# A switch-routed layer in one launch: the tokens at the boundary of two experts handled in blocks of 128 instead of 256

## What is computed

```python
xn = _layernorm(x)                                   # x: 8 x 512 x 512, that is 4096 tokens
s = attention(xn)                                    # 16 heads, causal, alibi bias
logits = x_flat @ w_router.T                         # 2 experts
top_idx = jnp.argmax(probs, axis=-1)
h = jnp.einsum('nd,ehd->enh', x_flat, w_fc)          # 512 -> 2048, per expert
a = jnp.square(jnp.where(h >= 0, h, 0.5 * h))
expert_out = jnp.einsum('enh,edh->end', a, w_proj)   # 2048 -> 512
out = jnp.einsum('end,en->nd', expert_out, mask * top_weight[None, :])
x = x + s * silu(out)
```

## Time and profile before

| | us |
|---|---|
| median of 3 runs (1542.73 to 1542.98) | 1542.82 |
| the profiled execution | 1544.06 |
| its span | 1542.0 |
| PE busy in the span | 1416.1 |
| DVE busy | 936.1 |
| ACT busy | 775.3 |
| POOL busy | 692.2 |

### The profile page before, as it was taken

One profiled execution on the slowest core, in us unless ns is written; L12 is line 12 of the kernel. 1 busy time (PEld: TensorE's weight loads), 2 busy tenths in 40 slices (PEclk: granted clock), 3 DMA queues, 4 the chain that ended last, 5 costly groups with the idle time before them and its releaser, 6 DMA issues. The chain is left out here.

```text
span 1542.0 us, 30070 instructions
## 1 busy us (share of the span) xinstructions
PE 1416.1 (92%) x9912; PEld 897.1 (58%) x9912; DVE 936.1 (61%) x2432; ACT 775.3 (50%) x1826; POOL 692.2 (45%) x900
## 2 busy tenths in 40 slices
PE   2879999999999999998659999999999999999995
PEld 1445565656555555655336666666666666666663
DVE  7577777777777676767449755555444445555542
ACT  3478787777777777787336422222222222222221
POOL 0456557474655656465323433333333333333331
PEclk9999999999999999999869999999999999999998
DMA  4425335343433424333157311111000111111000
GB/s 154 144 76 165 96 104 157 98 145 97 138 104 125 134 92 140 115 106 115 31 178 243 113 42 42 42 42 42 29 28 27 30 42 42 42 42 42 28 15 28
DMA packets 85136, 133.97 MB, mean 87 GB/s; under 512 B 14207, under 2 KB 63359, under 8 KB 82816
## 3 DMA queue, kind: packets, MB, share of 16 engines
q1 hardware_dynamic: 75808, 105.70, 21.3%
q0 software_dynamic: 9184, 26.36, 5.4%
HBM read 98.34 MB, written 34.21 MB: 86 GB/s over the span
## 5 line engine op out<-in xcount | busy, mean ns | idle before, releaser
L1010 PE MATMUL psF<-xT,wf 128*128 128x256 f16 x3264 | 380.7, 274 | 6.7 <-DVE wf L1113 6.7
L1028 PE MATMUL psY<-wf,aT 128*128 x1632 | 374.1, 379 | 0.0
L1010 PEld LDWEIGHTS psF<-xT,wf 128*128 x3264 | 320.4, 98 | 73.9 <-issue 7.4
L1216 POOL TENSOR_TENSOR a<-a 128x512 f32<-128x512 f32 x136 | 157.4, 1157 | 408.1 <-DVE a L1130 406.5
L864 POOL TENSOR_SCALAR pr<-pr,rden 128x128 f32<-128x128 f32 (+3 forms) x512 | 269.0, 544 | 137.2 <-DVE rden L794 135.9
L554 ACT ACTIVATE pr<-pr,mn 128x128 f32<-128x128 f32 (+3 forms) x512 | 281.8, 553 | 0.0
L1028 PEld LDWEIGHTS psY<-wf,aT 128*128 128x128 f16 x1632 | 159.7, 98 | 163.6
L783 DVE CUSTOM_DVE_ANT_0 pr<-psS,base,nsl 128x128 f32<-128x128 f32 (+3 forms) x512 | 250.0, 544 | 2.3 <-PE psS L410 1.9
L431 PE MATMUL psT<-conf,pr 128*128 128x128 f32 x1280 | 207.9, 281 | 23.1 <-POOL pr L864 19.2
L1064 ACT ACTIVATE rl<-psF 128x512 f32<-128x512 f32 x136 | 81.1, 596 | 265.0 <-PE psF L1010 265.0
L337 PE MATMUL psA<-xT,wqkv 128*128 128x512 f16 x768 | 196.7, 395 | 15.5 <-DVE wqkv L636 13.1
(11 more groups left out here) (137 smaller groups left out, 1382.7 us busy)
## 6 DMA issues: line engine op xcount, KB each, us to landing
qk_parts<-pre SPq DMA_DIRECT2D x64, 256.0 KB, 2.2
qs<-qk_parts SPq DMA_DIRECT2D x128, 128.0 KB, 2.6
ks<-qk_parts SPq DMA_DIRECT2D x128, 128.0 KB, 2.6
wst<-in_wf SPq DMA_DIRECT2D x16, 1024.0 KB, 6.3
wstage<-in_wf SPq DMA_DIRECT2D x32, 512.0 KB, 4.6
xin<-in_x SPq DMA_DIRECT2D x32, 256.0 KB, 4.0
attn_out<-so SPq DMA_DIRECT2D x32, 256.0 KB, 2.0
pt<-in_wqkv SPq DMA_DIRECT2D x4, 768.0 KB, 10.3
```

Source lines behind the costliest of these rows:

```text
L1010: last = nc.tensor.matmul(psF[c % 2][:, k * TT:(k + 1) * TT], w(e, 2 * hc, hl, kc * 512 + col, P), xT[:, r % 2, x, kc, :], start=(m == 0), ...
L1028: last = nc.tensor.matmul(psY[r % 2][h][:], aT[:, c % 4, x, k, h * P:(h + 1) * P], w(e, 2 * hc + 1, hl, q * 512, 512), start=(c == 0 and k ...
L1216: nc.gpsimd.tensor_tensor(at, at, at, ALU.mult).then_inc(s["a_ready"], 1)
```

## The change

The block at the boundary is now 128 tokens. With n0 the number of tokens of expert 0, `n0[1]` is n0 rounded down to 128 and `n0[2]` is its 128 bit. There are 16 slots of 256 tokens and, last, one of 128, 4224 tokens in all where 4352 were before. If the 128 bit is 0, the last slot handles the boundary block for expert 0; if it is 1, the 256-token slots of expert 1 begin 128 tokens earlier, and the last slot handles the last 128 tokens of the table for expert 1. So `tint` now counts in blocks of 128, and `mall` has one row for each of these. `halves(n)` is 2, and 1 for the last slot, and stands wherever a loop ran over `NH`: ups with 128 moving columns, six products in a down, one transpose set, one gather of x and of s, one scatter, half as wide operations in the chain. The expert of slot 0 can now be expert 1 (if n0 is under 128). So `eint` counts experts in the order of use, and SP reads from `ebase` which of the two experts' weights to load first; it computes the address of every weight load from it. The diff, cut (the last slot's `halves(n)` in the loops of ACT, DVE and POOL is left out where it only replaces `NH`):

```diff
-    c[:, C_SLOT:C_SLOT + SLOTS] = TT * np.arange(SLOTS)[None, :]
+    c[:, C_SLOT:C_SLOT + SLOTS] = TT * np.arange(SLOTS)[None, :] + P
...
+            LAST = SLOTS - 1
+            setup(ts(n0[:, 0:1], esum[:, 0:1], -1.0, float(TOK), ALU.mult, ALU.add))
+            setup(ts(n0[:, 0:1], n0[:, 0:1], float(TOK - 1), None, ALU.min))
+            setup(nc.vector.tensor_copy(n0i[:, 0:1], n0[:, 0:1]))
+            setup(ts(n0i[:, 1:2], n0i[:, 0:1], P, None, ALU.bitwise_and))
+            setup(ts(n0i[:, 0:1], n0i[:, 0:1], TOK - P, None, ALU.bitwise_and))
+            setup(nc.vector.tensor_copy(n0[:, 1:3], n0i[:]))
+
             setup(ts(eslot[:], conf[:, C_SLOT:C_SLOT + SLOTS], n0[:, 0:1], None, ALU.is_gt))
-            setup(nc.vector.tensor_copy(eint[:], eslot[:]))
-            setup(nc.vector.scalar_tensor_tensor(out=tint[:], in0=conf[:, C_SLOT:C_SLOT + SLOTS], scalar=1.0 / TT,
-                                                in1=eslot[:], op0=ALU.mult, op1=ALU.subtract))
+            setup(ts(eslot[:, LAST:SLOTS], n0[:, 2:3], 1.0 / P, None, ALU.mult))
+            setup(ts(n0[:, 3:4], n0[:, 1:2], -1.0, float(TOK - P), ALU.mult, ALU.add))
+            setup(ts(tf[:], eslot[:], n0[:, 2:3], -1.0, ALU.mult, ALU.mult))
+            setup(nc.vector.tensor_tensor(tf[:], tf[:], conf[:, C_SLOT:C_SLOT + SLOTS], ALU.add))
+            setup(ts(tint[:], tf[:], 1.0 / P, -1.0, ALU.mult, ALU.add))
+            setup(ts(tf[:, 0:1], eslot[:, LAST:SLOTS], n0[:, 3:4], n0[:, 1:2], ALU.mult, ALU.add))
+            setup(ts(tint[:, LAST:SLOTS], tf[:, 0:1], 1.0 / P, None, ALU.mult))
+
+            setup(ts(eint[:], eslot[:], eslot[:, 0:1], None, ALU.not_equal))
+            setup(ts(ebase[:, 0:1], eslot[:, 0:1], 2.0 * HC, None, ALU.mult))
+            setup(ts(ebase[:, 1:2], eslot[:, 0:1], -2.0 * HC, 2.0 * HC, ALU.mult, ALU.add))
...
+def halves(n):
+
+    return 1 if n == SLOTS - 1 else TT // P
...
-            return (n - (r % ring) + ring) * (16 * NH // ring)
+            return (n - (r % ring) + ring) * (16 * NH // ring) - 16 * (NH - halves(n))
...
+        def part(t, n):
+
+            return t.rearrange("p (k n) -> p k n", k=2)[:, :, 0:halves(n) * P]
...
+            stored_as = [sp.value_load(ebase[0:1, e:e + 1], min_val=0, max_val=NP) for e in range(E)]
             for k, n in enumerate(order):
                 if k >= RING:
                     sp.wait_ge(s["ws_lo"], k - RING + 1)
                 c = n % 2 * HP
-                sp.dma_start(wstage[:, k % RING, :], io["wf"][n // 2, :, c:c + HP]).then_inc(w_in[k % RING], 16)
+                sp.dma_start(wstage[:, k % RING, :], io["wf"][bass.ds(stored_as[n // 2 // NP] + n // 2 % NP, 1), :, c:c + HP]
+                             .rearrange("o p n -> (o p) n")).then_inc(w_in[k % RING], 16)
...
-                    wait(pe, s["X_lo"], (n + 1) * NH)
+                    wait(pe, s["X_lo"], n * NH + halves(n))
                 if n < PRE:
                     wait(pe, s["ws_lo"], arrival[4 * (n * HC + hc) + 1])
                 wait(pe, s["f_sum"], t - 1)
+                tn = halves(n) * P
                 for k in range(2):
                     col = (2 * (c % 2) + k) * P
                     m = 0
                     for hl, parts in ((0, (0, 1)), (1, (0,))):
                         for kc in range(KC):
                             for x in parts:
-                                last = nc.tensor.matmul(psF[c % 2][:, k * TT:(k + 1) * TT],
-                                                        w(e, 2 * hc, hl, kc * 512 + col, P), xT[:, r % 2, x, kc, :],
+                                last = nc.tensor.matmul(psF[c % 2][:, k * TT:k * TT + tn],
+                                                        w(e, 2 * hc, hl, kc * 512 + col, P), xT[:, r % 2, x, kc, 0:tn],
...
-                        for h in range(NH):
+                        for h in range(halves(n)):
...
-                    if c in (1, 3) and ahead:
+                    if c in (1, 3) and ahead and (c - 1) // 2 < halves(n + 1):
...
-                tile = dve.value_load(tint[0:1, bass.ds(n, 1)], min_val=0, max_val=TOK // TT - 1)
-                src = mall[:, bass.ds(tile, 1), :].rearrange("p o c -> p (o c)")
-                nc.vector.tensor_copy(rec[:, r % 4, :], src)
-                nc.vector.tensor_copy(gidx[:, r % 4, :], src.rearrange("p (h c) -> p h c", c=MROW)[:, :, 0]
+                tile = dve.value_load(tint[0:1, bass.ds(n, 1)], min_val=0, max_val=TOK // P - halves(n))
+                src = mall[:, bass.ds(tile, halves(n)), :].rearrange("p h c -> p (h c)")
+                nc.vector.tensor_copy(rec[:, r % 4, 0:halves(n) * MROW], src)
+                nc.vector.tensor_copy(gidx[:, r % 4, 0:halves(n)], src.rearrange("p (h c) -> p h c", c=MROW)[:, :, 0]
...
-                        at = a[:, cu % 2, :]
+                        at = part(a[:, cu % 2, :], nu)
```

More of the change, by code:

```diff
@@ L1063, in relu @@
                 wait(act, s["f_sum"], t - 1)
-                nc.scalar.activation(rl[:, c % 2, :], psF[c % 2][:], ACT.Relu, scale=2.0 ** -28
+                nc.scalar.activation(part(rl[:, c % 2, :], n), part(psF[c % 2][:], n), ACT.Relu, scale=2.0 ** -28
                                      ).then_inc(s["f_relu"], 1)
@@ L1070, in ahi @@
                 wait(act, s["Y_done"], t - 3)
-                nc.scalar.activation(aT[:, c % 4, 0, :, :].rearrange("p k n -> p (k n)"), a[:, c % 2, :], ACT.Copy
+                nc.scalar.activation(aT[:, c % 4, 0, :, 0:halves(n) * P], part(a[:, c % 2, :], n), ACT.Copy
                                      ).then_inc(s["U_hi"], 1)
@@ L1076, in step @@
                     split(weights_due(n, c))
-                    if c in (2, 4) and within(n + 1, 0, SLOTS):
+                    if c in (2, 4) and within(n + 1, 0, SLOTS) and (c - 2) // 2 < halves(n + 1):
                         h = (c - 2) // 2
@@ L1091, in step @@
                     if c == 0 and within(n - 1, 0, SLOTS):
-                        for h in range(NH):
+                        for h in range(halves(n - 1)):
                             wait(act, s["z_ready"], (n - 1) * NH + h + 1)
@@ L1129, in total @@
                 wait(dve, s["U_hi"], t - 1)
-                nc.vector.scalar_tensor_tensor(out=a[:, c % 2, :], in0=psF[c % 2][:], scalar=2.0 ** -28,
-                                               in1=rl[:, c % 2, :], op0=ALU.mult, op1=ALU.add
+                nc.vector.scalar_tensor_tensor(out=part(a[:, c % 2, :], n), in0=part(psF[c % 2][:], n),
+                                               scalar=2.0 ** -28, in1=part(rl[:, c % 2, :], n),
+                                               op0=ALU.mult, op1=ALU.add
                                                ).then_inc(s["f_sum"], 1)
@@ L1185, in step @@
                                 op0=ALU.mult, op1=ALU.add).then_inc(s["o_ready"], 1)
-                        dve.wait_ge(s["o_ready"], n * NH)
+                        dve.wait_ge(s["o_ready"], (n - 1) * NH + halves(n - 1))
                     if c == 0 and within(n + 2, 0, SLOTS):
                         fetch(n + 2, r + 2)
-                    if c in (0, 2) and within(n + 1, 0, SLOTS):
+                    if c in (0, 2) and within(n + 1, 0, SLOTS) and c // 2 < halves(n + 1):
                         h, r1 = c // 2, (r + 1) % 4
@@ L1196, in step @@
                            rec[:, r1, h * MROW + 4:h * MROW + 5], ALU.subtract, ALU.mult).then_inc(s["ln_done"], 1)
-                assert not done or k[0] == LK, k[0]
+                assert not done or k[0] == 2 + halves(n - 1), k[0]
             slots(dve, step)
@@ L1202, in _, with gather @@
         def _(pool):
-            def gather(dst, src, r, sm):
-                for h in range(NH):
+            def gather(dst, src, n, r, sm):
+                for h in range(halves(n)):
                     nc.gpsimd.indirect_dma_start(
```

33 lines of the change are left out of this document (17 added, 16 removed).

## The result

The changed kernel takes 1520.68 us (median of 4 runs, 1519.17 to 1521.90), where the kernel before took 1542.78 (median of 4). The ratio is 0.985 with a 95% interval of 0.9838 to 0.9862. Forecast: 1521.0 us, range 1518.0 to 1525.0.

A forecast was written before the change was run, and what follows sets the result against it. PE was taken to bound the experts' part, busy 590.19 of 591 us. The terms -20.6 - 0.4 - 2.5 + 1.0 + 0.7 = -21.8 us, from the median of 1542.82, gave 1521.0 us, range 1518.0 to 1525.0.

The forecast's parts named there:

- The half slot: Last slot on PE: ups of 1.34 us and downs of 1.30, eight of both saving 20.6 us.
- Rival 1: Last slot's ups: weight loads at 98 ns pace narrow products, 2.35 us an up, 1528.1 us in all; chance 0.10.
- Late downs: End of the last slot: the last down waits for the elementwise chain, +1.0 us, bounds 0 and +2.3.
- the disturbance by slot 15's scatters: Start of last slot: full-width scatters on POOL, 7.7 to 10.4 us in, hold up square 4.
- A turn of the ring: Last slot's chain of alo, total, square, ahi and relu: 2.1 us, under the step's 2.64.
- the gather: POOL in the last slot: it ends at 12.3 us, between square 4 (11.1) and square 5 (13.0).
- Rival 2: Last slot: POOL's square stays at 1.04 us, the last downs wait 2.3 us, 1522.3 us in all; chance 0.12.
- Transposes: PE in slot 15: one set of four transposes goes, saving 0.4 us.
- The tail: Behind the last product: less scaling and product with s, one scatter gone, -2.5 us, bounds -1.8 and -3.1.
- The seam: At 768 us: DVE's longer closing chain costs 0.2 us, later weight loads 0.5; +0.7 us together.
- The sum: Whole kernel: all terms together -21.8 us, 1521.0 us from the median, 1.4% faster.
- slower granted clock at the first product: First product at 128 columns: a possible slower clock, left out of the forecast since PE stays as busy; no size.

The follow-up runs named there:

- e3: Changed kernel with every up of all 17 slots done in products of 128 columns; 1528.67 us, ratio to before 0.9907.
- e1: Changed kernel with the last slot 256 tokens wide again, new routing and computed addresses kept; 1545.7 us, ratio to before 1.0006.
- e8: Changed kernel with slot 15's two scatters put one behind square 4 and one behind square 5; 1520.97 us, ratio to before 0.9851.
- e4: Changed kernel with SP's weight loads at fixed addresses, expert 0 first; 1522.19 us, ratio to before 0.9854.
- e0: The changed kernel run again unaltered, for the spread of its times and a second trace; 1522.15 us, ratio to before 0.9857.

## Why the prediction was right, point by point

**The half slot.** Ups of 1.34 us and downs of 1.30: as forecast, and e3 shows the 55.9 ns in a sustained stream. Rival 1 is out.

**Late downs.** Forecast +1.0, measured 0.7: the last slot takes 27.16 us where the products in it (eight ups of half width, slot 15's last two downs and eight downs of half length) and 0.2 us to the scaling would take 26.45. The chain "in the long run keeps up" and the disturbance by slot 15's scatters are as told, piece by piece. Counted from PE's step 0 (1482.45), the first scatter starts at 7.6 us (7.7 forecast), the second ends at 10.3 (10.4), square 4 at 10.9 (11.1), square 5 at 12.9 (13.0) and alo of step 7 at 17.65 (18.1). A turn of the ring is 1.93 us (from square 6 at 1496.65 to square 7 at 1498.58), 2.1 were forecast. Two pieces were off. The half-wide square takes 0.61 us alone, under the 0.69 that I scaled:

```profile
1498.58 0.61 POOL L1245 TENSOR_TENSOR a<-a 128x256 f32<-128x256 f32 x1 [1.32 <-DVE a L1158]
```

And the gather wasn't the cause, but one of two conditions at a tie. Rival 2 (a square of 1.04 us) is out by the same row, though beside DVE's 128x512 operations it takes 0.99.

**Transposes.** Forecast -0.4, measured -0.46 (676.35 to 675.89, the stretch that lost them).

**The tail.** Forecast -2.5, bounds -1.8 to -3.1, measured -3.3 against before and -3.1 against e1. This is the term that was mis-sized, and against before it lies outside its bounds. What had to go ahead of the scatter went as told: the first scatter starts 5.35 us behind the first scaling in e1 and 4.19 after, 1.2 us less. Before it was 5.60, with a pause of DVE that e1 doesn't show, the 0.29 us of this row of before:

```profile
1526.48 0.69 DVE L1182 SCALAR_TENSOR_TENSOR z<-gt,sg 128x512 f32<-128x512 f32 x1 [0.29 <-DVE oidx L1178]
```

What I missed is the scatter itself: the first of two takes 1.40 us, and I kept that for the single one, which takes 1.01. Before, DVE worked on the second half's rows beside it. In e8 the scatters of slot 15, which start in pauses of DVE, take 1.03 and 1.04 us instead of 1.40 and 1.01. The last 0.2 us lie behind the last scatter: from its end to the end of the span it is 10.56 us before and 10.54 in e1, with two scatters, and 10.35 after, with one. So the 0.8 us that the term lacked are 0.4 of scatter, 0.2 of closing and 0.25 of a pause that only the trace of before has.

**The seam.** Forecast +0.7. DVE reaches the meeting 0.3 us behind SP, 0.2 was forecast. SP's first weight load starts 1.8 us behind the meeting where it was 0.3 (770.86 against 770.6), 1.5 us later where 1.7 were forecast, but the 0.5 us that the gathers should lose by it don't show by the third up (e4). Counted to the third up, the stretches sum to 34.00 us before and 34.10 after.

**The sum.** By stretches it is +0.1 - 0.46 - 19.9 - 3.3 = -23.6 us, and I had -21.8. The medians differ by 22.1, and e1 and e0 by 23.5. That the forecast lies 0.3 us from the measured median is partly luck, then: the terms were 1.8 us short (late downs 0.3, transposes and products 0.1, tail 0.8, seam 0.6), all in the same direction, and the medians show 1.5 us less than the stretches do, which is within what the attention part alone moves by. The prediction named a slower granted clock at the first product and left it out; a dip of it does come, behind the third up's start, and costs each later trace 1.4 us there, in e1 with its full last slot as in the changed kernel, so it isn't of the change's making.

## What to carry to other kernels

When an engine is busy all the time, price a change by the pace of its groups (start to start), and price narrower work by extrapolating between two widths in the trace; then look at what the narrower work no longer covers, since a chain with room for 10 us suddenly has 5. When an edit at one of two suspected waits moves nothing, both may end at the same moment: take both away before dropping either. And judge an effect of a microsecond by a stretch of the trace between two fixed points, not by medians that a part elsewhere shakes by five, and when such a stretch itself differs by a microsecond, look at the granted clock in it first.

## What the runs showed of the hardware

- Products of 128 x 128 weights with 128, 256 and 512 moving columns, each with its own weight load, follow each other at 55.9, 109.2 and 215.8 ns at 2.4 GHz (granted clock 1.00), with weight loads shown at 98 ns hidden throughout.
- An indirect DMA is issued by POOL in 1.0 us. A scatter that starts during DVE's last row operation (L1184) takes 1.38 to 1.40 us in 17 of 17 cases before, and one that starts during `alo` (L1137) 1.01 in 14 of 14, so it isn't DVE's work as such that slows it.
- A POOL product of 128 x 256 takes 0.61 us alone and 0.99 beside DVE's products and row operations of 512 columns; one of 128 x 512 takes 1.04 us alone, 1.42 beside those, and up to 2.02 beside DVE's splitting of weights (L1141).
- The granted clock fell to 0.50 for 3.4 us within busy stretches of PE, and not in every trace: about 1 us behind the third up in 12 of 14 traces (1.4 us lost), and within the last outputs of attention in 4 of 14 (3.1 us with what goes before it). The steps of slots 2 to 15 are 5.21 us in traces with the first dip and in those without.
- The attention part took 764.0 to 771.2 us up to its end in 14 traces, the changed kernel alone 764.6 to 770.0 in three. Up to 3.1 us of it go with the dip, and 4 us are there by 181 us; what makes those is open, no experiment here was on it.
